# Softmax sums by two columns of ones, and scores clipped in their PSUM bank, in the attention stage of a layer kernel

## What is computed

```python
def _L0_attn_ref(x, W_DQ, W_UQ, W_QR, W_DKV, W_UK, W_UV, W_KR, W_O):
    ...
    q = jnp.concatenate([q_C, q_R], axis=-1)
    ...
    k = jnp.concatenate([k_C, k_R], axis=-1)
    v = (c_KV @ W_UV.T).reshape(B, S, H, D_H).transpose(0, 2, 1, 3)
    d_qk = D_H + D_HR
    scores = jnp.einsum('bhqd,bhkd->bhqk', q, k)
    scores = jnp.clip(scores, -80.0, 80.0)
    causal = pos[:, None] >= pos[None, :]
    scores = jnp.where(causal[None, None], scores, -jnp.inf)
    weights = jax.nn.softmax(scores / jnp.sqrt(jnp.float32(d_qk)), axis=-1)
    attn = jnp.einsum('bhqk,bhkd->bhqd', weights, v)
    out = attn.transpose(0, 2, 1, 3).reshape(B, S, H * D_H) @ W_O.T
    return out
...
xn = _layernorm(x, axis=-1)
x = x + _L0_attn_ref(xn, ...) + _L0_ffn_ref(xn, ...)
```

## Time and profile before

| | us |
|---|---|
| median of 3 runs | 1353.98 |
| lowest, highest | 1353.33, 1354.11 |
| the profiled execution | 1354.13 |
| its span in the trace | 1352.4 |

### The profile page before, as it was taken

The page is one execution under the profiler, slowest core; times in us unless marked ns, Lnnn a source line. Parts: engine busy times, 40 slices in busy tenths (PEclk is TensorE's granted clock), DMA queues, the critical chain, the costliest instruction groups (busy, mean ns, idle before and its releaser), DMA issues.

```text
span 1352.4 us, 21141 instructions
## 1 busy us (share of the span) xinstructions
PE 1313.1 (97%) x6553; PEld 1085.1 (80%) x6553; DVE 741.2 (55%) x1365; ACT 620.2 (46%) x1146; POOL 629.5 (47%) x534
## 2 busy tenths in 40 slices
PE   5999999999999999999998999999999999999998
PEld 3778888778888888888886788888888888888887
DVE  6361165232222222222224678888888888788876
ACT  6421143222222222222225566666676667667664
POOL 5125584994060003200001476677666776676553
PEclk9999999999999999999999899999999999999999
DMA  8125552664241213311115124323242323322012
GB/s 274 54 106 199 191 182 77 184 185 133 64 148 56 63 53 105 108 50 62 59 37 179 39 46 79 76 44 82 39 92 46 72 62 64 76 40 61 17 47 95
DMA packets 72953, 123.25 MB, mean 91 GB/s; under 512 B 10960, under 2 KB 19280, under 8 KB 72848
## 3 DMA queue, kind: packets, MB, share of 16 engines
q1 hardware_dynamic: 42000, 60.49, 15.5%
q0 software_dynamic: 11312, 27.23, 9.3%
q10 hardware_dynamic: 19536, 34.17, 7.7%
HBM read 74.41 MB, written 39.05 MB: 84 GB/s over the span
## 4 chain that ended last, share of the span: by engine, by line
PE 88%; POOL 6%; DVE 2%; issue 1%; DMA 1%; ACT 1%; POOLq 0%; SPq 0%; ACTq 0%; DVEq 0%
PE bank L48 79%; PE bank L1648 4%; POOL slots L523 3%; PE bank L1440 2%; POOL slots L521 2%; PE bank L1381 1%; PE bank L1557 1%; DMA rows_b<-in_x 1%; PE bank L1367 0%; DMA rot_sin<-sum_b 0%; POOL slots L467 0%; DVE stats L886 0%; PE bank L1501 0%; POOL store_a L529 0%; POOLq L523 0%
## 5 line engine op out<-in xcount | busy, mean ns | idle before, releaser
L48 PE MATMUL bank<-store_b,store_a 128*128 128x512 f32 (+1 forms) x1536 | 324.6, 363 | 6.7 <-DVE store_b L1249 3.2
L48 PE MATMUL bank<-slots,x_turned 128*128 x1296 | 324.2, 399 | 6.1 <-POOL slots L523 3.9
L48 PEld LDWEIGHTS bank<-store_b,store_a 128*128 128x128 f32 x1536 | 255.0, 190 | 60.3 <-issue 8.7
L48 PEld LDWEIGHTS bank<-slots,x_turned 128*128 128x128 f32 x1296 | 235.8, 188 | 66.9 <-issue 22.9
L932 DVE TENSOR_TENSOR hid_t<-bank,hid_t 128x512 fp32r<-128x512 f32 x70 | 48.4, 691 | 357.7 <-ACT hid_t L651 357.7
L48 PE MATMUL bank<-slots,hid_t 128*128 (+1 forms) x840 | 208.6, 397 | 3.4 <-DVE hid_t L932 3.4
L48 PEld LDWEIGHTS bank<-slots,hid_t 128*128 128x128 f32 x840 | 153.5, 188 | 34.8 <-DVE hid_t L932 2.1
L48 PE MATMUL bank<-store_b 128*128 128x512 f32 x768 | 179.4, 389 | 0.0
L48 PEld LDWEIGHTS bank<-store_b 128*128 128x128 f32 x768 | 144.1, 188 | 29.9
L521 POOL CAST slots<-staging 128x512 f32 (+1 forms) x84 | 51.5, 613 | 182.0 <-PE bank L48 180.2
L825 ACT ACTIVATE p_store<-bank 128x512 f32<-128x512 f32 x160 | 95.6, 598 | 85.9 <-PE bank L48 84.4
(11 more groups left out here) (204 smaller groups left out, 1825.3 us busy)
## 6 DMA issues: line engine op xcount, KB each, us to landing
staging<-in_w SPq DMA_DIRECT2D x56, 256.0 KB, 2.8
sorted_y<-y_store ACTq DMA_DIRECT2D x54, 256.0 KB
rows<-sorted_x ACTq DMA_DIRECT2D x51, 260.0 KB, 2.7
rot_sin<-sum_b SPq DMA_DIRECT2D x128, 64.0 KB, 2.0
staging<-in_wg SPq DMA_DIRECT2D x28, 256.0 KB, 2.8
shared_y<-y_store ACTq DMA_DIRECT2D x16, 256.0 KB
raw<-in_wot SPq DMA_DIRECT2D x16, 256.0 KB, 2.8
acc<-in_x SPq DMA_DIRECT2D x16, 256.0 KB, 5.4
```

Of the source, the lines that this page charges most:

```text
L48: made = pe.matmul(out, a, b, start=first and n == 0, stop=last and n == len(pairs) - 1, skip_group_check=onto)
```

## The change

**Clipping.** VectorE now reads the scores in their bank, clips at +-80 and writes `p_store`; masked places get -30000. ScalarE then takes the exponential in place in `p_store`. So the order is clip, exponential, round, where it was exponential, clip, round. A scores bank is free after the clip, where it was free after the exponential, and the waits for a free place in `p_store` move from ScalarE's queue to VectorE's.

**Sums.** `sum_a` goes. TensorE holds two columns as the stationary operand (ones and zeros, or zeros and ones) and streams the rounded probabilities of groups 0 and 2 into row 0, and `sum_b`, which ScalarE now rounds and POOL takes the low part of, into row 1: six products. The sums stand in two rows of a bank. ScalarE copies them to `divisor_rows`, SP sends them by two DMAs of 16 bytes a partition to `sum_store`, one query on each partition, and VectorE inverts from there. The inversion moves behind clip 4 in VectorE's queue.

Lines shift: L48 is L49 after, the clips L1275 and L1280 are L1299 and L1304, the exponential L825 is L842, the rescale L833 is L849.

```diff
+        unit = tile(ctx, "unit", [P, 2, 2])
+        unit_r = tile(ctx, "unit_r", [P, 2, 2], F32R)
+        sum_store = tile(ctx, "sum_store", [P, 2, 2, 2, 2])
...
-                pe.wait_ge(on["exps_done"], NG * n[0] + n[1] + 1)
+                pe.wait_ge(on["clipped"], NG * n[0] + n[1] + 1)
...
-                pe.wait_ge(on["ratio_made"], n[0] + 1)
-
-        def prob_slot_free(act, u, g):
+                pe.wait_ge(on["rows_made"], n[0] + 1)
+
+        def prob_slot_free(dve, u, g):
 
             n = NG * u + g - (NG + 1)
             if n < 0:
-                act.wait_ge(on["y_done"], NBK)
+                dve.wait_ge(on["y_done"], NBK)
                 return
             v, f = divmod(n, NG)
-            act.wait_ge(on["sum_step"], 4 * v + 4)
+            dve.wait_ge(on["sum_step"], 3 * v + 3)
...
+                sp.wait_ge(on["rows_made"], u + 1)
+                if u >= 2:
+                    sp.wait_ge(on["ratio_made"], u - 1)
+                for s in range(2):
+                    sp.dma_start(sum_store[:, u % 2, s].rearrange("p h t -> p (h t)"),
+                                 divisor_rows[s:s + 1, :].rearrange("o (p c) -> o p c", p=P)).then_inc(
+                        on[f"divisor_sent{u % 2}"], 16)
...
-            pool.memset(cap[:], float(np.exp(CLIP * SCALE))).then_inc(on["cap_filled"], 1)
+            pool.memset(cap[:], CLIP).then_inc(on["cap_filled"], 1)
             pool.wait_ge(on["cap_filled"], 1)
-            pool.affine_select(out=cap[:, 0:P], in_=cap[:, 0:P], compare_op=ALU.is_ge, fill=0.0, base=0,
+            pool.affine_select(out=cap[:, 0:P], in_=cap[:, 0:P], compare_op=ALU.is_ge, fill=LATER, base=0,
                                pattern=[[1, P]], channel_multiplier=-1).then_inc(on["cap_made"], 1)
-            pool.memset(one[:], 1.0).then_inc(on["one_made"], 1)
+            pool.memset(unit[:], 0.0).then_inc(on["unit_made"], 1)
+            pool.wait_ge(on["unit_made"], 1)
+            for s in range(2):
+                pool.memset(unit[:, s, s:s + 1], 1.0).then_inc(on["unit_made"], 1)
...
-                pool.wait_ge(on["clipped"], NG * u + 3)
-                pool.tensor_tensor(sum_a[:], w[0][:, :, P:2 * P], w1_q1, ALU.add).then_inc(on["sum_step"], 1)
                 if u + 1 < NU:
                     sine(u + 1)
-                pool.wait_ge(on["clipped"], NG * u + 4)
+                pool.wait_ge(on["exps_done"], NG * u + 4)
                 pool.wait_ge(on["cosine_done"], min(u + 2, NU))
                 pool.tensor_tensor(sum_b[:], w[1], w[3], ALU.add).then_inc(on["sum_step"], 1)
-                pool.wait_ge(on["clipped"], NG * u + 5)
-                pool.wait_ge(on["sum_step"], 4 * u + 2)
+                pool.wait_ge(on["exps_done"], NG * u + 5)
+                pool.wait_ge(on["sum_step"], 3 * u + 1)
                 pool.tensor_tensor(sum_b[:], sum_b[:], w[4], ALU.add).then_inc(on["sum_step"], 1)
-                pool.wait_ge(on["sum_step"], 4 * u + 3)
+                pool.wait_ge(on["sum_step"], 3 * u + 2)
                 pool.tensor_tensor(sum_b[:, :, P:2 * P], sum_b[:, :, P:2 * P], w3_q3, ALU.add).then_inc(
                     on["sum_step"], 1)
                 if u + 1 < NU:
                     rotate(u + 1)
+                pool.wait_ge(on["sums_high"], u + 1)
+                pool.tensor_tensor(sum_b_lo, sum_b[:], sum_b_hi.bitcast(F32), ALU.subtract).then_inc(
+                    on["sums_low"], 1)
...
             def round_high(u, g):
-                act.wait_ge(on["clipped"], NG * u + g + 1)
+                act.wait_ge(on["exps_done"], NG * u + g + 1)
                 if u:
                     act.wait_ge(on["dens_done"], u)
                 act.activation(p_hi[g], prob(u, g), ACT.Copy).then_inc(on["p_high"], 1)
 
             def exponents(u, g):
-                act.wait_ge(on["scores_done"], NG * u + g + 1)
-                prob_slot_free(act, u, g)
-                act.activation(prob(u, g), ring.bank("scores", u, g), ACT.Exp, scale=SCALE).then_inc(
-                    on["exps_done"], 1)
+                act.wait_ge(on["clipped"], NG * u + g + 1)
+                act.activation(prob(u, g), prob(u, g), ACT.Exp, scale=SCALE).then_inc(on["exps_done"], 1)
...
                 round_high(u, 4)
+                act.wait_ge(on["sum_step"], 3 * u + 3)
+                act.activation(sum_b_hi, sum_b[:], ACT.Copy).then_inc(on["sums_high"], 1)
...
+                act.wait_ge(on["dens_done"], u + 1)
+                if u:
+                    act.wait_ge(on[f"divisor_sent{(u - 1) % 2}"], 32 * ((u - 1) // 2 + 1))
+                act.activation(divisor_rows[:].rearrange("s (p c) -> s c p", p=P),
+                               ring.bank("sums", u)[0:2, :].rearrange("s (c p) -> s c p", p=P), ACT.Copy).then_inc(
+                    on["rows_made"], 1)
...
-                low, high = float(np.exp(-CLIP * SCALE)), float(np.exp(CLIP * SCALE))
-                dve.wait_ge(on["exps_done"], NG * u + g + 1)
-                w = prob(u, g)
+                dve.wait_ge(on["scores_done"], NG * u + g + 1)
+                prob_slot_free(dve, u, g)
+                w, bank = prob(u, g), ring.bank("scores", u, g)
                 if g in (1, 3):
-                    made = dve.tensor_scalar(w, w, low, high, ALU.max, ALU.min)
+                    made = dve.tensor_scalar(w, bank, -CLIP, CLIP, ALU.max, ALU.min)
                 else:
                     dve.wait_ge(on["cap_made"], 1)
                     n = P if g == 2 else 2 * P
-                    part = w.rearrange("p (h t) -> p h t", t=n)
-                    made = dve.scalar_tensor_tensor(part, part, low, cap[:, 0:n].unsqueeze(1).broadcast_to(
+                    part, scored = (v.rearrange("p (h t) -> p h t", t=n) for v in (w, bank))
+                    made = dve.scalar_tensor_tensor(part, scored, -CLIP, cap[:, 0:n].unsqueeze(1).broadcast_to(
                         [P, BANK // n, n]), ALU.max, ALU.min)
                 made.then_inc(on["clipped"], 1)
...
-                sums = ring.bank("sums", u)[:, 0:8].rearrange("p (n h t) -> p n h t", n=2, h=2)
-                dve.wait_ge(on["dens_done"], u + 1)
-                dve.reciprocal(inv_store[:, u % 2], sums).then_inc(on["inverted"], 1)
+                dve.wait_ge(on[f"divisor_sent{u % 2}"], 32 * (u // 2 + 1))
+                dve.reciprocal(inv_store[:, u % 2], sum_store[:, u % 2]).then_inc(on["inverted"], 1)
                 dve.wait_ge(on["inverted"], u + 1)
-                dve.tensor_tensor(ratio[:, u % 2], inv_store[:, u % 2, :, 0], sums[:, :, 1], ALU.mult).then_inc(
-                    on["ratio_made"], 1)
+                dve.tensor_tensor(ratio[:, u % 2], inv_store[:, u % 2, :, 0], sum_store[:, u % 2, :, 1],
+                                  ALU.mult).then_inc(on["ratio_made"], 1)
...
             for u, (p, b) in enumerate(units):
-                if u:
-                    invert(u - 1)
                 clip(u, 0)
                 clip(u, 1)
                 if u + 1 < NU:
                 take_low(u, 1)
                 clip(u, 3)
                 clip(u, 4)
+                if u:
+                    invert(u - 1)
                 take_low(u, 2)
...
-                pe.wait_ge(on["one_made"], 1)
-                first = prob(u, 0).rearrange("p (h t) -> p h t", h=2)
-                for tt in range(TB):
-                    if tt:
-                        pe.wait_ge(on["sum_step"], 4 * u + (1, 4, 4)[tt - 1])
-                    for h in range(2):
-                        w = (first[:, h, 0:P], sum_a[:, h, :], sum_b[:, h, 0:P], sum_b[:, h, P:2 * P])[tt]
-                        n = 4 * (tt // 2) + 2 * h + tt % 2
-                        made = pe.matmul(ring.bank("sums", u)[:, n:n + 1], w, one[:, 0:1], start=True, stop=True)
-                made.then_inc(on["dens_done"], 1)
+                pe.wait_ge(on["unit_rounded"], 1)
+                row = ring.bank("sums", u)[0:2, :]
+                second_half = row.rearrange("p (h t) -> p h t", h=2)[:, :, P:2 * P]
+                product(pe, row, [(unit_r[:, 0, :], s[0]) for s in (p_hi, p_lo)], last=False)
+                product(pe, second_half, [(unit_r[:, 0, :], s[2][:, 0:2 * P].rearrange("p (h t) -> p h t", h=2))
+                                          for s in (p_hi, p_lo)], first=False, last=False)
+                pe.wait_ge(on["sums_low"], u + 1)
+                product(pe, row.rearrange("p (h t) -> p h t", h=2),
+                        [(unit_r[:, 1, :], sum_b_hi), (unit_r[:, 1, :], sum_b_lo)], first=False).then_inc(
+                    on["dens_done"], 1)
```

26 lines of the change are left out of this document (15 added, 11 removed).

## The result

The changed kernel takes 1383.1 us (median; 1381.62 to 1384.35) where the kernel before takes 1353.98: a ratio of 1.0216, with an interval of 1.0202 to 1.023. It is slower by 29.1 us; forecast were 1383.6. The profiled execution's span is 1382.1 us (1352.4 before), the mean granted TensorE clock 0.998.

What follows compares the result with a forecast made beforehand. TensorE was taken to bound the kernel. Sums -18.2, stall +45.3 and the end's divisors +2.4 make +29.5 us on the profiled execution's 1354.13: forecast 1383.6 us, range 1361 to 1397.

Steps and rivals of the forecast that it cites:

- What bounds the kernel: Whole kernel: TensorE works 1313.1 of 1352.4 us, so only what it does or newly waits for moves the end.
- The sums on TensorE: Each attention unit: products of 1.71 us become 1.14, a gain of 0.57 us a unit, 18.2 us over 32.
- Rival 4: Sums on TensorE: narrow products cost as much as wide weight loads, 18.2 not gained, 1402 us; chance 0.02.
- The order clip, exponential, round: Attention units: ScalarE and VectorE wait in turns, so TensorE's output products end at T+14.82, not T+13.36 (T: unit's start).
- The stall: TensorE's output products, waiting for ScalarE's rescales: 1.46 us in every unit from the second, 31 times, 45.3 us.
- The divisors: Row copy and two DMAs after the sums: hidden in units with 4 us to spare, +2.4 us once at the end.
- the working of the end: After the last sums: 0.2 + 0.6 + 3.3 + 0.4 + 0.66 to rescale 0's end, making TensorE 2.4 us late.
- Rival 1: Attention units: VectorE gets faster, clips are early enough, kernel faster than before, 1350.1 or 1338.3 us; chance 0.11.
- Rival 3: Attention units: late divisors or late low part of the sums, each further us paid per unit, 1415 us; chance 0.06.

Runs made afterwards that it cites:

- the last one with both edits: Changed kernel with group 1's low part behind clip 4, experts' additions behind the next unit's inversion and rotation copy ahead of exponential 1: 1354.51 us, ratio 1.0.

## Why the prediction was right

**What bounds the kernel.** Right: what TensorE does and newly waits for is the whole difference, and in the units it newly waits in one place.

**The sums on TensorE.** Right. 1.16 us a unit against the 1.14 forecast and the 1.71 of the earlier trace rows; the kernel with the sums alone gained 18.52 - 17.93 = 0.59 a plain unit, forecast 0.57. Rival 4 is out: a stationary operand of two columns costs no more than one of 128. In all the sums alone gave 16.3 us, less than 18.2, as they pay a longer end: 11.42 us from their last sums to the last instruction, where 9.57 were before.

**The order clip, exponential, round.** The mechanism is right link by link. Forecast and read: exponential 2 at T+5.81 and T+5.71; low part 6.99 and 6.89; clip 3 7.60 and 7.50; rescale 0 10.98 and 10.83; head 1 11.68 and 11.63. The stall is 1.08 + 0.40 = 1.48 here, and 19.39 - 17.93 = 1.46 as the difference of two kernels; 1.46 was forecast. The clip out of the bank, unseen in the trace of before, takes what the row gave it (shortest, median, longest ns):

```profile
L1299 DVE TENSOR_SCALAR p_store<-bank x64: 676/684/692, 738.4 to 1358.4; 128x512 f32<-128x512 f32 x64
...
L1304 DVE SCALAR_TENSOR_TENSOR p_store<-bank,cap x96: 673/683/693, 737.3 to 1359.0; 128x512 f32<-128x512 f32 x96
```

The 419 ns of the earlier trace rows is gone from all 64. The Trainium skill, "VectorE: DVE Perf Modes", Mode 2×_2P, says that it needs its operands in SBUF; the runs agree, 676 ns being the shortest.

**Per unit 0.84, not 0.89.** This is a small error of the base: the unit whose timeline was read is one of the shortest. The plain units of before run from 18.52 to 18.82, and the last period, with no next unit to prepare, lost only 0.63. With the first of the 31 stalls inside the start, the units hold 25.1 - 0.55 = 24.5 us, where 45.3 - 18.2 = 27.1 were forecast.

**The divisors.** Hidden in the units, as forecast. In the working of the end two terms were off and offset each other. ScalarE's copy of two rows takes not 0.6 but 1.06 us (1047 to 1091 ns in 32), although it moves 1024 numbers; the two DMAs take 2.67 us from its end to VectorE's inversion, not 3.3. ScalarE, then VectorE (answers to the earlier trace rows):

```profile
1369.52 1.06 ACT L900 ACTIVATE divisor_rows<-bank 2x512 f32<-2x512 f32 x1 [0.50 <-PE bank L49]
1373.74 2.39 ACT L849 ACTIVATE bank<-bank,ratio 128x512 f32<-128x512 f32 x4 [3.16 <-DVE ratio L1327]
```

```profile
1373.25 0.20 DVE L1325 RECIPROCAL inv_store<-sum_store 128x8 f32<-128x8 f32 x1 [3.50 <-DMA sum_store<-divisor_rows]
```

So TensorE waits 1374.55 - 1369.33 - 2.72 = 2.50 us, forecast 2.4. But the end became 3.2 us longer, and the rest is a step that the prediction did not have:

```profile
1369.33 2.92 PE L49 MATMUL bank<-store_b 128*128 128x512 f32 x12
1374.55 4.32 PE L49 MATMUL bank<-store_b 128*128 128x512 f32 x12 [2.30 <-ACT bank L849]
```

The second twelve take 4.32 us. The stretches around them show why (first the window and its length; then busy us and instructions of TensorE, its weight loads, VectorE, ScalarE, POOL; the granted clock; DMA share and GB/s):

```profile
1372.20:1374.50 2.30, 0.05 (x1) 0.00 (x0) 0.36 (x2) 0.76 (x2) 0.00 (x0) 1.00 0.03 1
1374.50:1376.00 1.50, 1.45 (x6) 1.25 (x7) 0.47 (x1) 1.50 (x3) 0.00 (x0) 0.97 0.00 0
1376.00:1379.00 3.00, 2.87 (x7) 1.66 (x6) 1.87 (x4) 0.13 (x1) 0.00 (x0) 0.50 0.46 175
```

TensorE stood idle for 2.3 us and began again near full clock (0.97); in the next stretch the granted clock was 0.50, the lower level of 1.2 GHz. In the kernel before, with no such gap, the stretch from 1345.0 to 1348.6 was granted 1.00 throughout, and 24 products took 5.73, or 2.87 for twelve. The low clock so cost about 1.4 us in this execution; what stands behind the products is 0.6 shorter (3.23 against 3.84). 2.5 + 1.4 - 0.6 is the 3.2 within 0.1. The stall of 1 us in each unit did not lower the clock: the mean over the span is 0.998.

The low clock is not a fixed price of that gap. Twelve of the kernels here have it, in one of them 4.9 us long (the two without are the one before and the clips alone). In eight the clock fell and the last twelve products took 4.3 to 5.3 us; in four (the sums alone, the changed kernel with the early rotation, the divisors behind the swap, and the last one with both edits) it stayed at 1.00 behind the same 2.3 us, and they took 2.98 to 3.03. What decides between the two is open.

**Not forecast:** the 1.95 us ahead of the second unit's sums. 1.86 of them lie ahead of the attention stage, which starts later as a whole. The traces show that this start is not steady: in the eleven kernels that clip in the bank VectorE's first clip starts anywhere from 736.14 to 738.75 (737.27 in the changed one), though, but for a few small fills, they do the same work ahead of it; and in the kernel before the scores were first read at 735.44. Why is open. So the hit to 0.5 us is partly luck: the terms were off by -2.6 (units), +1.95 (start) and +0.8 us (end), and the last holds 1.4 us of low clock that other kernels with the same gap did not pay.

**The rivals.** Rival 1 had half of its premise right: no clip stretched any more, 693 ns at most against 1784 in the earlier trace rows, and the clips' busy time fell from 137.0 to 109.5 us. But VectorE's load as a whole did not fall (742.6 us against 741.2 in the earlier trace rows): the ratio went from 5.1 to 23.9 us and the low parts of groups 1 to 4 from 125.2 to 129.4. It had its conclusion wrong, as the prediction said: the chain is made of waits and not of load. Rival 3, the late low part of the sums, did not come in this kernel. It came in two neighbours, where POOL's rotation had been put ahead of its additions. The prediction was too dear here: it had the low part end by T+18.2 and late by 0.7 us without the stall, and it ended at T+16.9, and in time without the stall (the wait for it in the kernel with the sums alone is 1.1 us, once).

## What to carry to other kernels

Two in-order engines that hand results to each other twice in a unit make a chain whose length is the sum of both, and each stands idle in it however much work it has elsewhere; when an operation changes its place from behind to ahead of another engine's, write out the turns with their times and compare the end with the next reader's margin. Each link can be priced and taken out by order alone, and a shift at the first link arrives whole at the last; but three of the reorderings here (the low part behind the clips, that with the early rotation, and both edits at last) freed one wait and met the next, so they are tried together and apart. The best kernel was half of the change: the sums by two columns of ones with the clips left behind the exponentials, 1338.8 us.
